# A projection taken three steps later in the next row block, and loads moved behind the last transposes

## The reference

```
q = x @ Wq.T + bq;  k = x @ Wk.T + bk;  v = x @ Wv.T + bv
a = q @ k.T / sqrt(512) + adj + adj
x = layernorm(x + softmax(a) @ v)

h = relu(adj @ (x @ W1) + b1)
x = layernorm(x + adj @ (h @ W2) + b2)
```

## Time and profile before

| | |
|---|---|
| median of 3 runs | 2142.36 us (2140.28 to 2143.95) |
| profiled execution | 2146.57 us, span 2144.8 us |
| PE busy | 1971.7 us (92%) |
| DVE busy | 1055.7 us (49%) |
| ACT busy | 824.6 us (38%) |
| DMA queue of SP | 456.92 MB, 85.6% of the 16 engines' span |
| mean granted TensorE clock | 0.967 of full |

### The profile page before, as it was taken

One profiled execution on the slowest core, in us unless ns is written; L12 is line 12 of the kernel. 1 busy time (PEld: TensorE's weight loads), 2 busy tenths in 40 slices (PEclk: granted clock), 3 DMA queues, 4 the chain that ended last, 5 costly groups with the idle time before them and its releaser, 6 DMA issues.

```text
span 2144.8 us, 25788 instructions
## 1 busy us (share of the span) xinstructions
PE 1971.7 (92%) x8976; PEld 884.7 (41%) x8976; DVE 1055.7 (49%) x2028; ACT 824.6 (38%) x1844; POOL 123.1 (6%) x201
## 2 busy tenths in 40 slices
PE   6999999999998999999989999998999779899998
PEld 3444444444443444444434444443444334334443
DVE  7766565555555455555554555555555420001223
ACT  2454454444444444444444444444444311001112
POOL 0000000000000000000000000000000000001334
PEclk8999999999999999999999999999999889999999
DMA  8465698999899888989988899889998979999996
GB/s 269 74 143 101 146 228 189 197 201 202 202 210 203 200 190 204 203 199 204 208 207 192 193 206 210 202 202 202 206 193 202 233 204 377 363 369 316 394 394 227
DMA packets 822324, 475.36 MB, mean 222 GB/s; under 512 B 667920, under 2 KB 672144, under 8 KB 821936
## 3 DMA queue, kind: packets, MB, share of 16 engines
q1 hardware_dynamic: 812976, 456.92, 85.6%
q10 hardware_dynamic: 9216, 16.78, 2.1%
HBM read 225.25 MB, written 94.18 MB: 149 GB/s over the span
## 4 chain that ended last, share of the span: by engine, by line
PE 77%; DMA 10%; DVE 6%; SPq 5%; issue 1%; ACT 0%; POOL 0%; POOLq 0%; ACTq 0%; DVEq 0%
PE bank L412 12%; PE bank L414 12%; PE bank L413 12%; PE bank L492 9%; PE bank L493 9%; PE bank L494 9%; DMA x1T<-x1s 5%; PE bank L561 4%; PE bank L562 4%; PE bank L563 4%; SPq L323 2%; DMA tsp<-tsp 2%; DMA xv<-at_dram 1%; SPq L395 1%; PE bank L530 1%; DVE tsp L790 1%
## 5 line engine op out<-in xcount | busy, mean ns | idle before, releaser
L898 DVE SCALAR_TENSOR_TENSOR ring<-bank,sc,adj_in 128x512 f32<-128x512 f32 x256 | 192.2, 751 | 607.5 <-PE bank L414 602.6
L647 ACT ACTIVATE tsp<-ring 128x512 f16<-128x512 f32 x256 | 161.2, 630 | 825.6 <-DMA tsp<-tsp 825.4
L492 PE MATMUL bank<-xv,tsp 128*128 128x512 f16 x1024 | 408.9, 399 | 13.0 <-DMA tsp<-tsp 13.0
L493 PE MATMUL bank<-xv,tsp 128*128 128x512 f16 x1024 | 407.7, 398 | 0.0
L494 PE MATMUL bank<-xv,tsp 128*128 128x512 f16 x1024 | 405.5, 396 | 0.0
L412 PE MATMUL bank<-xT,gT 128*128 128x512 f16 x1024 | 388.1, 379 | 0.0
L413 PE MATMUL bank<-xT,gT 128*128 128x512 f16 x1024 | 388.1, 379 | 0.0
L414 PE MATMUL bank<-xT,gT 128*128 128x512 f16 x1024 | 388.1, 379 | 0.0
L790 DVE SCALAR_TENSOR_TENSOR tsp<-adj_in,s_a,tsp 128x512 f16<-128x512 f32 x256 | 190.3, 743 | 42.3 <-ACT tsp L655 42.1
L640 ACT ACTIVATE ring<-ring,bias 128x512 f32<-128x512 f32 x256 | 180.9, 706 | 7.4 <-DVE bias L915 7.4
L655 ACT ACTIVATE tsp<-adj_in,s_a 128x512 f16<-128x512 f32 x256 | 180.7, 706 | 0.4 <-DVE s_a L787 0.4
(11 more groups left out here) (145 smaller groups left out, 1976.5 us busy)
## 6 DMA issues: line engine op xcount, KB each, us to landing
adj_in<-in_adj SPq DMA_DIRECT2D x256, 256.0 KB, 3.3
at_dram<-tsp SPq DMA_DIRECT2D x256, 256.0 KB, 3.1
xv<-at_dram SPq DMA_DIRECT2D x60, 1024.0 KB, 15.5
xT<-at_dram SPq DMA_DIRECT2D x32, 1024.0 KB, 14.6
adj_in<-at_dram SPq DMA_DIRECT2D x21, 1024.0 KB, 14.3
xv<-in_x SPq DMA_DIRECT2D x8, 1024.0 KB, 13.5
g_dram<-tsp SPq DMA_DIRECT2D x32, 256.0 KB, 4.0
gT<-g_dram SPq DMA_DIRECT2D x32, 256.0 KB, 3.6
```

The source lines that it names most:

```text
L492: pe.matmul(dst, ah, vh, start=(kb == 0 and j == 0), stop=False)
L493: pe.matmul(dst, ah, vl, start=False, stop=False)
L898: dve.scalar_tensor_tensor(t, s_bank[s % S_BANKS][:, :], col["k_l"], adj_in[:, s % AR, :], ALU.mult, ALU.add).then_inc(v_add, 1)
```

## The change

The y product of row block r - 3, its two halves and its store move from kb = 0, 1, 2 to kb = 3, 4, 5. The load of `y_hl` moves from SyncE's step 256 to step 265, behind the last transpose of probabilities, and the loads of units 0 to 3 move from steps 257 to 260 to steps 266 to 269 (LO_LAG is 10).

```
-STATS_AT, NORM_AT, X1_AT, XT_AT, Y_AT, YOUT_AT, RES_AT = 4, 5, 6, 6, 0, 1, 2
+STATS_AT, NORM_AT, X1_AT, XT_AT, Y_AT, YOUT_AT, RES_AT = 4, 5, 6, 6, 3, 4, 5
...
-                if s == NS:
+                if s == NS + LO_LAG - 1:
                     sp.wait_ge(p_qk, NS)
                     for i in range(2):
                         sp.wait_ge(d_y[i], 16 * len(range(i, Y_DRAM, 2)))
                     sp.dma_start(y_hl[:, 0:Y_DRAM, :, :].rearrange("p t two f -> p t (two f)"),
                                  y_dram[0:Y_DRAM].rearrange("t p n -> p t n")).then_inc(d_yin, 16)
-                if NS < s <= NS + 4:
-                    load_unit(s - NS - 1)
+                if NS + LO_LAG <= s < NS + LO_LAG + 4:
+                    load_unit(s - NS - LO_LAG)
```

## The result

The changed kernel takes 1983.88 us (median of 4 runs, 1982.85 to 1984.18), the one before 2141.32 on the same chip: ratio 0.9262, 95% interval 0.9246 to 0.9278. 1983 was predicted.

The account below looks back on a forecast made before the run. TensorE was taken as bound by waits for x1T (118.5 us idle) and the half clock behind them; 151 + 13 - 5 = 159 us off the 2142.4 median gives 1983, 8 in 10 range 1968 to 2010.

Parts of the forecast that it names:

- Rows: Attention row blocks: moving the y product three steps later removes TensorE's wait for x1T and the half clock, gaining 151 us.
- the 5.21 us: Per row block, period 47.33 minus work 42.12 us: about 3.6 us idle time and 1.6 us half clock.
- the 1.6 us: Per row block, time lost at half clock behind the x1T wait, claimed to go with that wait.
- Rival 2: In the rows, half clock stays though idle time goes: gain 104 + 8, time 2030 us; chance 0.04.
- all the others: Rows: DMA sets pace (0.07), y_lo wait reaches TensorE (0.03), x1T wait stays (0.03), DMA ceiling makes it slower (0.05).
- Margin of x1T: At the moved y product, TensorE comes 15.5 us later for x1T that was 3.5 late: 12 us to spare.
- What is late next: In the rows, transposed probabilities at full pace: at least 4 us margin, 227 GB/s fits narrowly, cost 0.
- y_hi and y_lo: In each row, VectorE's y_lo waits 1.3 us for ScalarE's y_hi, delaying p_lo 1.6 us; hidden, cost 0.
- End of attention: Nine steps from transpose 246 to 255 shrink from 55.7 to 42.6 us with the loads behind them: gain 13.
- its other bound (18): End of attention, upper bound: steps of 3.9 us since no adj loads are left, 37 in all, gain 18.
- What the later loads cost: Start of adjacency products: unit 4 starts about 7 us later, less about 2 of overlap; loss 5, bounds 0 and 11.
- Sum: Whole kernel: 151 + 13 - 5 = 159 us gained, median from 2142.4 to 1983 us.

Follow-up runs that it names:

- loads_late_only: Kernel before with only the loads of y and units 0 to 3 moved behind the last transposes, y product left: 2135.3 us, ratio 0.9962.

## Why the prediction was right

**Rows, 151 us predicted.** 151.8 between the two traces; the kernel with that part alone gained 151, some 2 of them at the end of attention. The work of a row was read off correctly (42.12 against 42.11), and both parts of the 5.21 us went. That the 1.6 us were half clock behind the idle time was argued then and is shown now: filling the wait brought the clock to 1.00 (1.45 us a row). Rival 2 is excluded by the clock of 1.00, and all the others by the rows of 42.11.

**Margin of x1T.** 12 us were predicted, and the median in the changed kernel is 11.95. One step of 5.18 us was enough too, with 0.6 us to spare at the tightest; the other two steps bought margin and no time.

**What is late next: nothing, but for a reason that was only half seen.** The cost of 0 was right, and so was the rate, 227 GB/s predicted and 226 measured. The prediction called the fit narrow by the bytes, against 231 GB/s, and the bytes had reserve to 251. For the queue it took the pace of the early stretch, 4.5 us a step against 5.18, and did not add the transfers of x1T, x, x1, y and g. SyncE's queue is the resource with less reserve: half a microsecond more a step costs 45 us. The prediction came out because the change adds nothing to that queue in the rows.

**y_hi and y_lo.** Predicted: y_lo waits 1.3 us for y_hi. It did not. ScalarE and VectorE at kb = 4 in the profile after:

```profile
1009.49 0.26 ACT L675 ACTIVATE y_st<-bank 128x128 f16<-128x128 f32 x1
```
```profile
1013.50 0.15 DVE L948 TENSOR_SCALAR veps<-mv 128x1 f32<-128x1 f32 x1
1013.58 0.28 DVE L790 SCALAR_TENSOR_TENSOR y_st<-bank,y_st 128x128 f16<-128x128 f32 x1
1013.77 0.71 DVE L790 SCALAR_TENSOR_TENSOR tsp<-ring,tsp 128x512 f16<-128x512 f32 x1
```

y_hi is done 4 us before y_lo starts here, and 3.5 to 5.6 us before it in all 29 row blocks; y_lo costs VectorE 0.2 us. ScalarE's place relative to VectorE was taken from the profile before, where it was later in its step; in the profile after the order of the two has changed. That the stall in the row had made the old order is likely and not shown. The transposes did come nearer to their use, for example 8.5 us (issued at 1494.72, used at 1503.18) where I had found 10.1:

```profile
1494.72 1.24 SPq L312 DMA_TRANSPOSE tsp<-tsp  x1
```
```profile
1503.18 0.38 PE L492 MATMUL bank<-xv,tsp 128*128 128x512 f16 x1
```

This one follows the x1T and x transfers in the queue, so it is not y_lo's doing. The shortest such distance in the rows is 7.5 us (9.6 before), a microsecond less than predicted. The longest landing is still 5.9 us, and the margin held: the tightest transpose landed 3.4 us ahead of its use.

**End of attention, 13 us predicted.** 17.9. The mechanism was right (13.9 to 15.8 of it go with the loads), the step was mis-sized: 4.2 us a step, x1T and x included, where 4.5 plus 2 in all were taken. The pace of the early stretch has an adj load in each step, which is absent at the end; the prediction had this in its other bound (18).

**What the later loads cost, 5 us predicted.** 6.0. The wait at the start of the adjacency products is 6.88 us, about 6 were predicted. x1T was issued at 1587.83, behind y, four units and the store of x, and landed only after them, 10.3 us later (median 3.6); its product began at 1598.13, 24.1 us behind transpose 255, and the units went on at 1599.19, 25.2 behind. That was 8 us later than before, yet only 6 were lost, since the DMA stream and not TensorE sets the pace afterwards (share 1.07). By the Trainium skill's rule (DMA: Bandwidth & Descriptors, Queues, rings and completion order: each DMA engine takes descriptors in ring order) x1T lands behind the loads, and the trace agrees, with 24.1 and 25.2 us where the prediction had 24 and 25.

**Sum.** 159 predicted, 163.7 between the spans; most of the difference is the 5 us at the end of attention. That the time matched to 1 us is luck in part. The profiled execution of before was 5.3 us above its median, 4.2 above the median that the prediction started from. Most of this excess seems to lie in its rows: `loads_late_only`, the same program up to there, issued transpose 246 at 1683.65 and not at 1688.08, 4.4 us earlier. Against it the rows gain 147.4 and not 151.8 (an estimate from these two traces). So for a median execution the rows were predicted 2 to 4 us too high and the end of attention 5 too low, and the two nearly cancel. The sum of 159 is met by the medians, 157.4 apart on the first chip and 160.6 on a later one.

## What to carry to other kernels

Take the period of a loop twice, once from starts far apart and once from the sum of its matmuls: the difference is what a moved wait can give in the loop, here half again as much as the listed idle time. A product needs to move only as far as its operand is late, so one step of distance was enough here; before adding anything to such a loop, sum the issue time of the queue that feeds it, not only its bytes. Large loads that nobody needs yet went behind the last small transfers on the path (8.8 us faster), since most of their time then fell into a hole in the DMA engines' work; in small pieces among those transfers they were another 2 us better.

## What the runs showed of the hardware that I had not expected

A 2 KB copy (128 pieces) in each step on SyncE's queue cost 45.7 us, as much as 128 KB (47.0), while 128 KB from ScalarE's queue cost 1.4, no more than chips differ (all against 1983.63). A transpose issued directly behind the 1.9 MB load of y held SyncE's queue for 7.44 us instead of 1.24, and x1T behind y, four units and a store for 5.83. The mixture of transposes and copies was carried at 251 GB/s with nobody waiting, at a recorded DMA share of 1.11; a share of 1.0 is therefore no limit by itself. 16 added matmuls a row made a kernel 39 us faster, since they kept the clock at its 2.4 GHz level.
